# FFN weights freed of their row means, the last chunks' y loaded in two parts, and new slots

## What is computed

```python
def _layernorm(x, axis=-1, eps=1e-05):
    m = jnp.mean(x, axis=axis, keepdims=True)
    v = jnp.var(x, axis=axis, keepdims=True)
    return (x - m) / jnp.sqrt(v + eps)
...
x = x + 0.5 * _L0_ffn_ref(_layernorm(x), L0_ffn_W, L0_ffn_b, L0_ffn_V_r, L0_ffn_C)
x = x + _L0_attn_ref(_layernorm(x), L0_attn_W_attn, L0_attn_W_proj)
x = x + 0.5 * _L0_ffn_ref(_layernorm(x), L0_ffn_W, L0_ffn_b, L0_ffn_V_r, L0_ffn_C)
```

## Time and profile before

| | us |
|---|---|
| median of three runs | 1777.77 |
| lowest, highest | 1775.73, 1783.82 |
| own time of the profiled execution | 1776.91 |
| its span, first to last instruction | 1775.2 |
| TensorE busy | 1620.3 (91%) |
| ScalarE busy | 1379.9 (78%) |
| VectorE busy | 1349.2 (76%) |
| GpSimd busy | 1292.4 (73%) |

### The profile page before, as it was taken

One profiled execution on the slowest core, in us unless ns is written; L12 is line 12 of the kernel. 1 busy time (PEld: TensorE's weight loads), 2 busy tenths in 40 slices (PEclk: granted clock), 3 DMA queues, 4 the chain that ended last, 5 costly groups with the idle time before them and its releaser, 6 DMA issues.

```text
span 1775.2 us, 67710 instructions
## 1 busy us (share of the span) xinstructions
PE 1620.3 (91%) x27158; PEld 822.4 (46%) x27158; DVE 1349.2 (76%) x3229; ACT 1379.9 (78%) x2214; POOL 1292.4 (73%) x1455
## 2 busy tenths in 40 slices
PE   6787989999998999999998999999998999899994
PEld 3453444444445544444445544444455545344442
DVE  4767777878787787878887787887878677788881
ACT  2456768988887888888886888888887887788881
POOL 2566657777878896878878797877878787677662
PEclk9888999999999999999999999999999999999997
DMA  3653532432446443332436534243434535322211
GB/s 100 182 161 102 167 117 81 131 90 79 116 115 175 136 145 112 112 112 80 145 100 167 167 114 136 80 132 103 130 104 141 156 99 157 90 69 67 81 41 53
DMA packets 183222, 206.16 MB, mean 116 GB/s; under 512 B 27004, under 2 KB 156916, under 8 KB 181116
## 3 DMA queue, kind: packets, MB, share of 16 engines
q1 hardware_dynamic: 182908, 201.77, 39.2%
HBM read 123.65 MB, written 76.30 MB: 113 GB/s over the span
## 4 chain that ended last, share of the span: by engine, by line
PE 60%; DVE 15%; POOL 9%; ACT 8%; issue 5%; DMA 1%; SPq 1%; POOLq 0%; ACTq 0%; DVEq 0%
PE y_ps L1215 23%; PE score L1215 18%; PE bank L1215 16%; DVE rp L1148 9%; POOL rp L938 4%; ACT rp L1045 3%; PE bank L1241 3%; ACT rp L1065 2%; DVE lin L1154 2%; POOL z L900 2%; DVE bnst_ln L1173 1%; POOL rp L913 1%; PE bank L1280 1%; POOL lin L913 1%; ACT rp L1061 1%
## 5 line engine op out<-in xcount | busy, mean ns | idle before, releaser
L1148 DVE TENSOR_SCALAR rp<-score 128x512 f32<-128x512 f32 (+3 forms) x1728 | 973.1, 591 | 274.4 <-PE score L1215 272.5
L938 POOL TENSOR_TENSOR rp<-rp 128x1024 f32<-128x1024 f32 (+3 forms) x416 | 710.9, 1716 | 95.1 <-DVE rp L1148 82.5
L1215 PE MATMUL score<-qs,ks 96*32 96x512 bf16 (+3 forms) x10240 | 722.0, 352 | 51.8 <-DVE lin L1154 21.7
L1215 PE MATMUL y_ps<-rp,vt 128*16 128x512 f32 (+3 forms) x5120 | 599.5, 536 | 36.2 <-DVE lin L1154 12.2
L1045 ACT ACTIVATE rp<-score 128x512 f32<-128x512 f32 (+3 forms) x832 | 435.4, 561 | 203.8 <-PE score L1215 199.3
L1215 PEld LDWEIGHTS score<-qs,ks 96*32 96x32 bf16 x10240 | 299.1, 96 | 431.6 <-DVE rp L1148 161.2
L1061 ACT ACTIVATE rp<-rp,rise 128x1024 f32<-128x1024 f32 (+3 forms) x416 | 438.8, 1077 | 6.5 <-POOL rp L913 6.4
L913 POOL TENSOR_SCALAR_AFFINE_SELECT rp<-rp 128x256 f32<-128x256 f32 (+1 forms) x400 | 189.9, 475 | 262.0 <-ACT rp L1045 191.7
L1065 ACT ACTIVATE rp<-rp 128x2048 f32<-128x2048 f32 (+2 forms) x224 | 342.6, 1529 | 16.0 <-POOL rp L913 14.6
L1154 DVE SCALAR_TENSOR_TENSOR lin<-score,slope_mask 128x128 f32<-128x128 f32 x736 | 206.3, 280 | 0.0
L1215 PEld LDWEIGHTS y_ps<-rp,vt 128*16 128x16 f32 x5120 | 138.0, 96 | 133.6 <-issue 32.4
(11 more groups left out here) (80 smaller groups left out, 1293.6 us busy)
## 6 DMA issues: line engine op xcount, KB each, us to landing
ks<-part_scratch SPq DMA_DIRECT2D x648, 64.0 KB, 2.4
qs<-part_scratch SPq DMA_DIRECT2D x384, 64.0 KB, 2.3
part_scratch<-parts SPq DMA_DIRECT2D x14, 1536.0 KB, 5.9
vt<-v_scratch SPq DMA_DIRECT2D x103, 128.0 KB, 2.6
state_scratch<-st_new SPq DMA_DIRECT2D x16, 528.0 KB
x_sb<-in_L_attn_x_dram SPq DMA_DIRECT2D x16, 512.0 KB, 4.4
x_scratch<-x SPq DMA_DIRECT2D x16, 512.0 KB, 5.4
qT_scratch<-qkT SPq DMA_DIRECT2D x16, 512.0 KB, 3.3
```

Of the source, the lines that this page charges most:

```text
L938: pool.tensor_tensor(half, half, half, ALU.mult).then_inc(squared["pool"], 1)
L1148: nc.vector.tensor_scalar(rp[T % RP_BUFS][:, 2 * u + v, off:CH], score[H % S_BUFS][:, v, off:CH], 0.0, RISE, ALU.max, ALU.add).then_inc(ra ...
L1215: return nc.tensor.matmul(*args, start=start, stop=stop, skip_group_check=True)
```

## The change

1. The mean goes into the weights. (x - m) W^T equals x (W minus the mean of its rows)^T, so VectorE takes from each row of W and of V_r^T its mean in the setup. z1T and z3T then transpose x_sb and x2 themselves, and rstd is applied when VectorE evicts ffn and out, in two instructions of 256 columns for one of 512, since rstd is one number for each row. The z and shift of ln1 and ln3 are gone; ln2 keeps both. The bias is added to x in place when the transposes have read it.
2. The y of chunks 14 and 15 comes in parts: three head groups from the scratch together with x1c, the last group straight from y_sb.
3. Of the splits of the first four chunks GpSimd makes those with an odd index, with a buffer `rest` and a semaphore for each side.
4. Chunk 0: SP stores q's and k's first parts one after the other before it loads q, and the stores of v and qT to the scratch move behind.
5. z3T has a tile of its own; out_stored is one semaphore for each x2.
6. `WHOLE` and nearly all tables of slots are new.

```diff
-WHOLE = [1, 3, 6, 10, 16, 17, 20, 23, 26, 28, 31, 33, 35, 38]
+WHOLE = [1, 3, 6, 10, 14, 17, 20, 23, 26, 28, 30, 33, 35, 39]
...
-A_FULL = {"z1T": (32, 35), "ffn": (38, 40), "z2T": (64, 64), "ln1": 9, "ln2": 48}
+A_FULL = {"z1T": (30, 31), "ffn": (37, 39), "z2T": (64, 64), "ln1": 21, "ln2": 48}
...
-C_FULL = {"proj": (22, 26), "ln3": 31, "z3T": (67, 69), "out": (71, 75)}
+C_FULL = {"proj": (22, 26), "ln3": 58, "z3T": (67, 67), "out": (71, 75)}
...
-C_SHORT = {"proj": (0, 4), "ln3": 8, "z3T": (20, 21), "out": (22, 26)}
+C_SHORT = {"proj": (0, 4), "ln3": 9, "z3T": (9, 10), "out": (18, 22)}
...
-AGGR, SCALES, ROOT, NORM, BIAS = NB, NB + 4, NB + 2, NB + 5, 2 * NB + 5
+AGGR, SCALES, ROOT, NORM, BIAS = NB, NB + 4, NB + 2, NB + 5, NB + 5
...
+            def load_c_before(c):
+
+                for g in range(QUADS - 1):
+                    w = VISIT[c // CPB, g, c % CPB]
+                    sp.wait_ge(y_stored[w % 2], (w // 2 + 1) * (16 * QH))
+                sp.wait_ge(x1_stored, (c + 1) * 16)
+                wait_emptied(sp, "proj", c - 1, 1)
+                cols = slice(CH * c, CH * c + CH)
+                sp.dma_start(y_c[:, 0, :], y_d[0:P, cols]).then_inc(c_loaded, 16)
+                sp.dma_start(y_c[0:QD, 1, :], y_d[P:P + QD, cols]).then_inc(c_loaded, 16)
+                sp.dma_start(x1c[:], x1_d[cols, :].rearrange("(i p) d -> p i d", p=P)).then_inc(c_loaded, 16)
+
+            def load_c_last(c):
+
+                w = VISIT[c // CPB, QUADS - 1, c % CPB]
+                sp.wait_ge(y_copied, w + 1)
+                for h in range(QH):
+                    sp.dma_start(y_c[QD + HD * h:QD + HD * h + HD, 1, :],
+                                 y_sb[w % 2][STRIP * h:STRIP * h + HD, :]).then_inc(c_loaded, 16)
...
             def add_bias(k, x, ready, chunk, i):
                 if i == 0:
-                    pool.wait_ge(z_ready[k], chunk + 1)
+
+                    pool.wait_ge(job_done, o.made("z1T" if k == "ln1" else "z3T", chunk, 1))
+                    pool.wait_ge(stats_done[k], (chunk + 1) * NB)
...
                 for b, i, step in split_at.get(s, ()):
-                    if b >= EARLY and step != 1:
+                    if step != 1 if b >= EARLY else i % KC:
                         split(pool, b, i, step)
...
+            dve.wait_ge(ffn_loaded, 16 * 3)
+            nc.vector.tensor_reduce(w_mean[:], w_in[:], AX.X, ALU.add).then_inc(w_centred, 1)
+            dve.wait_ge(w_centred, 1)
+            nc.vector.tensor_scalar(w_mean[:], w_mean[:], -1.0 / DM, None, ALU.mult).then_inc(w_centred, 1)
+            dve.wait_ge(w_centred, 2)
+            for k in range(KC):
+                nc.vector.tensor_scalar(w_in[:, k, :], w_in[:, k, :], w_mean[:, k:k + 1], None, ALU.add).then_inc(w_centred, 1)
...
-                    nc.vector.tensor_tensor(x1[:, 2 * i:2 * i + 2, :], two, x_sb[:, 2 * i:2 * i + 2, :], ALU.add).then_inc(done, 1)
+                        dve.wait_ge(rstd_done["ln1"], a + 1)
+                    for j in range(2):
+                        blk = 2 * i + j
+                        ins = nc.vector.scalar_tensor_tensor(x1[:, blk, :], two[:, j, :], rstd["ln1"][:, blk:blk + 1], x_sb[:, blk, :],
+                                                             ALU.mult, ALU.add)
+                    ins.then_inc(done, 1)
...
                 if kind in ("z1T", "z2T", "z3T"):
-                    name = {"z1T": "ln1", "z2T": "ln2", "z3T": "ln3"}[kind]
-                    if first:
-                        pe.wait_ge(z_ready[name], a + 1)
-                    ins = transposes(dst, z3 if kind == "z3T" else z, i)
+                    if first and kind == "z1T":
+                        pe.wait_ge(x_loaded, (a + 1) * 16)
+                    if first and kind == "z2T":
+                        pe.wait_ge(z_ready, a + 1)
+                    if first and kind == "z3T":
+                        wait_emptied(pe, "proj", a, 1)
+                    ins = transposes(dst, {"z1T": x_sb, "z2T": z, "z3T": x2[a % 2]}[kind], i)
```

171 lines of the change are left out of this document (102 added, 69 removed).

## The result

The changed kernel takes **1712.4 us** (median of 4 runs, 1708.0 to 1713.4) against 1776.8 for the kernel before on the same chip (1773.2 to 1783.8): a ratio of 0.963, 95% interval 0.959 to 0.966. That is 64 us less. The prediction, 1747.5 us with a range from 1730 to 1766, was wrong, on the side of too little: the direction and the tail were right, the gains of the early stretch and of the middle were far too small, and the head cost more than forecast.

A forecast was written before the change was run, and what follows sets the result against it. It took TensorE's work plus its waits to bound the kernel; -11.8 - 2.3 + 3 - 3 - 16 = -30.1 us on a span of 1775.2 led to 1747.5 us, range 1730 to 1766 for 8 in 10.

The forecast's parts named there:

- z1T off the path: Early stretch: transposes no longer wait for GpSimd's z, -11.8 us; a fourth such stall at 1529.8 us, -2.3 us.
- I give back 40%: Early stretch: 40% of the 19.4 us from stalls and low clock is lost to splits moved to GpSimd; bounds 0% and 100%.
- My worry: Early stretch: GpSimd gets heavier by the moved splits, 27 us more against 9 us taken, each triple ahead of squares TensorE awaits.
- The fourth stall: At 1529.8 us: transposes waiting for GpSimd's z for 2.34 us, to go with nothing in its place, -2.3 us.
- The head: Before the first matmuls: VectorE's means of the weights' rows delay TensorE's start by 4.2 us; +3 us in all (0 to 5).
- so the delay shrinks to about 3 us there: Third visit: a first score some 5 us later becomes about 3 us, since TensorE already idled 2.99 us for keys.
- The middle: Steady chunks: lighter GpSimd and VectorE remove a little of 26 us of small TensorE waits, -3 us; bounds 0 and half.
- neither engine is full, so most such pieces come from the order of work and stay: Middle: most of TensorE's small waits for VectorE's evictions (14.6 us) and GpSimd's squares (11.5 us) remain.
- The tail: After the last y matmul: earlier load of y and no normalisation between projection and transposes, -16 us.
- Only the tail pays: Rival: SP's loads and GpSimd with the new splits set the early stretch; +3 - 16 = -13, about 1765 us; chance 0.20.
- A new wait of GpSimd: Rival: GpSimd waits for transposes before adding the bias, holding masks and squares; 39 us cost, 1786 us; chance 0.05.
- More than forecast: Rival: all 19.4 us stay, half the small waits go, tail -18; -50 us, about 1728 us; chance 0.17.

The follow-up runs named there:

- e_split: The changed kernel with all splits of qT and kT in the first four chunks back on VectorE: 1721.8 us.
- b_split: The kernel before with the splits of the second halves of qT and kT in the first four chunks moved to GpSimd: 1771.0 us, ratio 0.996.
- e_early: The changed kernel with the old slots of the first two chunks, ln1 moved so that the bias comes behind the transposes: 1708.3 us.
- e_shift: The changed kernel with the 32 shifts of ln1 and ln3 given back to VectorE as work nobody reads: 1726.2 us.
- e_both: The changed kernel with GpSimd's 128 normalising instructions and VectorE's 32 shifts given back as work nobody reads: 1742.9 us.

## Why the prediction was wrong, point by point

Stalls and copies of y don't fall together, so the terms are laid on the stretches first. The first stall of the earlier trace rows, at 93.88 us, lies before the 2nd copy, the other two between the 4th and the 12th, the fourth between the 48th and the 60th:

| up to the copy | 4th | 12th | 60th | end |
|---|---|---|---|---|
| forecast | +3 - 4.1 = -1.1 | -7.6 | -3 - 2.3 = -5.3 | -16 |
| measured | +1.4 | -21.3 | -26.5 | -18.0 |

**z1T off the path, -11.8 and -2.3 us: the working was right up to the last step.** The stalls of 13.1 us and the 6.3 us of low clock behind them went. Of these 19.4 us 12.7 lie between the 4th and the 12th copy, and 10.9 came there without the moved splits (e_split). The step that failed is "I give back 40%" for the splits moved to GpSimd. I had weighed 27 us of GpSimd against 9, and of VectorE's relief I had written only that it loses "some of its late evictions", without a number: it was late with scores and evictions itself, and its own splits were of the kind that GpSimd holds up. e_split has the move at 10.4 us of gain, not 7.6 of loss. My worry was true of the kernel before (b_split: one wait for z grows from 5.07 to 7.06 us), but the same change takes that wait away. Two edits were judged one by one where the first removes the cost of the second. The bounds were wrong in the same way: I had put the upper end at 0% given back. The fourth stall gave more than its 2.34 us, since TensorE ran at 0.66 of full speed from 1530 to 1535 us, some 1.7 us that I had left out.

**The head, +3 us: wrong, and hidden by the first stall.** The means cost 3.8 us (12.68 for 8.90 us; I had 4.2), the first score came at 61.41 (59 to 62). But the third visit came 8.0 us later, at 92.59, not at 86 to 89: the step that failed is "so the delay shrinks to about 3 us there". In the new slots z2T of chunk 1 waits 5.02 us for its z, a wait that the prediction doesn't have. By the 4th copy 1.4 us were left only because the first stall with its clock, 6.8 us, had gone in between. With the old early slots (e_early) the third visit is 1.4 us late and the 2nd copy 5.6 us ahead of the kernel before.

**The middle, -3 us: the step that failed most.** Measured 26.5 us from the 12th to the 60th copy, of which the fourth stall with its clock is some 4. I added the instructions' own time to get 26 us of engine time, said "neither engine is full, so most such pieces come from the order of work and stay", and capped the gain at half of the waits listed. Four things were wrong with it. I saw a shift take 661 ns on the mean and wrote that "it is held up by something else", but never asked what stands behind it in the queue when it is; e_shift shows it. I cut the list of the earlier trace rows at two entries and lost one of 12.2 us. I counted waits alone: TensorE idles 18.0 us less in this stretch and is busy 8.5 us less for the same matmuls, a part of it the clock (1.00 for 0.99). And idling and the order of work aren't apart: the order can be drawn tighter once the engines are lighter (old slots +36 us, old work +30 us, in the same kernel), so new slots are a part of the price of an edit.

**The tail, -16 us: right.** Last matmul of y to the end of the last eviction: 15.7 us (1688.05 to 1703.71), where it was 33.7. I had 17.9 us for the full-speed chain and chose 16; it is 18.0 (the table's 17.0 begin at the last copy of y, which now follows that matmul 1.0 us sooner). The projection starts 4.6 us behind the last matmul of y ("within 6") and takes 3.66 ("under 4"), transposes 0.14 us behind the eviction. The landing within the core, counted as I had counted it from the end of the last issue, took 1.36 us where I had 2.5, and the four issues 2.42 where I had 1.7: two errors that nearly cancel. From the start of its issue the last quarter took 1.95 us. The Trainium skill's page "DMA: Bandwidth & Descriptors", section "Anatomy of one DMA", names about 2.0 us as the fixed cost, there for transfers that GpSimd issues; the trace agrees if the count starts with the issue, and by the count of the prediction the 2.0 us were too much as well, if nearer. As I wrote, the bias is what is late next: VectorE waits 2.09 us for it ahead of out's first half, but the last half goes by TensorE.

**The rivals.** "Only the tail pays" fell with the 21.3 us before the 12th copy. "A new wait of GpSimd" did come: GpSimd waits 18.4 us in 11 pieces, up to 2.4, for the transposes ahead of ln1's bias (300 to 1700 us). But it isn't passed on: in that stretch no entry of TensorE's waits names the bias, and those for GpSimd's squares, which stand behind it, fell to 0.4 us. "More than forecast" (1728, 0.17) was the nearest and still 16 us short; its terms were the same capped waits. The prediction's sums have two slips that change nothing: 60% of 19.4 is 11.6, not 11.8, and 1746.8 + 0.9 is 1747.7, not 1747.5.

Still open: 7 of the 26.5 us of the middle that e_both doesn't give back. The fourth stall with its clock accounts for some 4, and e_both gives GpSimd 20 us less work back than the change took from it, and puts it ahead of the biases, not where the z stood; which share is whose wasn't tried apart. No run takes back the new `WHOLE` in the changed kernel, chunk 0's order of stores, or z1T's reading of x itself; that the last brings the 10.9 us is read from the stalls that are gone, not from a run without it.
